# Scores of two of nine steps through the two-bank ring, with one exponential of 1024 columns for two heads

## The chip, the cores and the metric

One core of one Trainium2 chip runs the whole kernel. The metric is device time in microseconds (us) of one execution; the median of three executions stands for the kernel. Engines: PE is TensorE (matmul; PEld its weight loads), DVE is VectorE, ACT is ScalarE, POOL is GpSimd, SP is SyncE, which issues the DMAs.

## What is computed

A transformer block with adaptive layer norm on x of shape (8, 1024, 256), in float32, with 16 heads of 16 channels and windows of 128 keys:

```python
h = layernorm(x) * (1 + ca) + sa
q, k, v = heads(h @ Wq.T + bq), heads(h @ Wk.T + bk), heads(h @ Wv.T + bv)
sc = q @ k.T / 4                               # 1024 x 1024 for each head
# inside each block of 128 keys, and under the causal mask: a softmax of its own
w = exp(sc - max_window(sc)); w = where(causal, w, 0)
w = w / sum_window(w)                          # 0 where the whole window is masked
p = softmax(w, axis=-1)                        # over all 1024 keys, masked ones count as exp(0)
x = x + ga * ((p @ v) @ Wo.T + bo)
h = layernorm(x) * (1 + cb) + sb
y = square(relu(h @ Wfc.T)) @ Wproj.T
x = x + gb * spikes(y) / 5                     # 5 steps of a spiking neuron, as a count of thresholds passed
```

So each score goes through two exponentials, with the window's sum and its inverse between them.

## The kernel before, in words

**Groups, units, steps.** A batch of 1024 tokens has 4 groups of 4 heads (`QH = 4`), 32 groups in all. A group's causal score blocks are cut into `NU = 9` units, each of 512 columns per head (`UNITS`, in transposed form: partitions are the 128 keys of a block, columns are queries). Step n brings the first stage of unit n; n goes to 287 (`NUNIT` = 288), with 14 steps of afterrun. s = n mod 9 is the unit inside the group: s = 0 the first step of a group, s = 8 the last. A batch is 36 steps.

**What runs in step n.** All engines follow the same step number, each with its own instruction stream, tied by semaphores. On TensorE, in this order (`step`, from L879): products of unit n-7 with V (L800, into `pv`); the window sums of unit n-1 (L790, `sum_unit`, which waits until all four first exponentials of step n-1 are done); for unit n-5 the inverse sums spread over the partitions (L829, `one_over_sums`, two calls, each filling one ring slot with two heads of 512 columns); in steps with s = 0 the rest of a mixed unit (`mixed_products`, also L800), ahead of which the first piece goes; then the scores of the four heads, `scores(n, 0..3)` (L775 matmul, L778 adds the causal mask), with other work set between them by tables: `piece` (below), `quantum` (L732, one matmul of the second feed-forward product), `maxima` (L750 and L753, scores in untransposed form of which VectorE takes the window maxima) and `turn_maxima` (L763), which turns the maxima so that SP can put them into the query stack by DMA (they are subtracted inside the score matmul). In step 7 of a group `outputs` (L838) turns the finished outputs.

On ScalarE: the second exponential of unit n-6 (L1046, 128x2048, all four heads), a logarithm and an exponential for the inverse sums (L1052, L1056, in steps divisible by 3), then the first exponentials, one for each head of 512 columns (L1041), with the pieces' evacuations between them. On VectorE: in steps with s = 0 and s = 6 the addition that takes `pv` (L1196), then the two products with the inverse sums, one for each ring slot of two heads (L1180, 128x1024), Newton's step for the inverse (L1184, L1186, steps divisible by 3), and the maxima (L1158), one for each ring slot. POOL splits operands (L1454 to L1458, L1488 to L1494), squares (L1467), counts spikes (L1479, L1481).

**Pieces.** Work of other batches is cut into pieces of one PSUM bank: T1, T2 (transposes before a projection, L664), QK (projections, four matmuls, L688; ScalarE takes them in two copies, L991 and L992), V, BH, BT, AT (turned attention output), O (output projection), F1 (eight matmuls of the first feed-forward product, L720; ScalarE takes it at L1014). The tables FRONT, BACK, NEAR, LATE and FIRST give for each step of a batch a first place (after head 0, or ahead of it where `piece_first`) and a last place (after head 3); QUANTA gives the numbers of quanta after each of the heads.

**PSUM.** There are two ring slots of two banks each (`ring`) and two score banks of one (`score`). Scores, turned maxima and all pieces go through the two score banks in turn: `score_slots` walks the whole order ahead of time and hands each item the bank and the item that held it before; `score_bank` (L644) waits for that item's reader. So head 2 waits for the exponential of head 0 where nothing stands between. The ring is used by the inverse sums (`"r"`, twice a step), the maxima (`"m"`, three a step in s = 1 to 6) and the turned outputs (`"o"`); `RING_NO` numbers them in order, `ring_slot` waits until the item two before was freed by VectorE (`ring_free`). In s = 0 and s = 8 the ring carries nothing but the two of the inverse sums. Semaphores: `st_ready` counts heads whose scores are ready, `e1_done` first exponentials, `ring_ready` filled slots, `ring_free` freed ones.

**SP** issues `load_stacks` for group g (q and k stacks, two DMAs) in step 9(g-1), after all scores of the group that used the same half of the stack.

Steps that the prediction names, with what is placed in them (one batch; the others repeat it every 36 steps):

- s = 8: step 107 F1 after head 0, then 0, 1, 1, 2 quanta after heads 0 to 3; step 116 AT after head 0, AT after head 3, quanta 1, 0, 1, 1; step 125 QK after head 0; step 134 F1 after head 3, quanta 0, 2, 3, 0.
- s = 0: step 108 one quantum after head 3; step 117 AT ahead of head 0, one quantum after head 3; step 126 T2 ahead of head 0 and T2 after head 3; step 135 F1 ahead of head 0 and F1 after head 3.
- at the beginning and the end: step 8 the turned maxima of group 1 between heads 1 and 2; 9, 27, 35, 36 and 269 nothing; 17 and 18 QK; 26 BT; 44 as 116 without quanta; 270 as 126.

## Time and profile before

| | |
|---|---|
| median of three executions | 2356.11 us (2353.27 to 2359.10) |
| the profiled execution | 2358.39 us, its span 2356.6 us |
| TensorE busy | 2206.2 us, 94% of the span |
| VectorE, ScalarE, POOL busy | 74%, 65%, 48% |
| mean granted TensorE clock | 0.99 |
| chain that ended last | PE 77%, DVE 10%, ACT 5%, POOL 4% |

The span runs from the first to the last instruction. A busy TensorE is not TensorE at its peak, since matmuls are pipelined and their ends are modelled. An engine's idle time matters only where the chain that sets the end passes through it; TensorE's waits are therefore what is to be read, and what ended each.

### The profile page before, as it was taken

Reading aid. Unit: us, or ns where it says so; the run is one execution under the profiler, and the core shown is the slowest. Engines: PE = TensorE matmul, PEld = TensorE weight load, DVE = VectorE, ACT = ScalarE, POOL = GpSimd, SP = SyncE. Lnnn points to the kernel's source line nnn. Section 1 sums busy time; section 2 is a strip of 40 time slices with the busy share of each in tenths; the row PEclk is TensorE's granted clock in tenths of the full one; section 3 lists DMA queues with packets and bytes.
Section 4 is the critical chain, followed back from the end, with each engine's and each line's share of the span. In section 5 each row is a group of like instructions: output and inputs, shape, how many; then the busy total and the mean of one; then the engine's idle time right before and its main releaser. Section 6 shows DMA issues by size and latency. Waiting matters only on the chain.

```text
span 2356.6 us, 46649 instructions
## 1 busy us (share of the span) xinstructions
PE 2206.2 (94%) x19164; PEld 1247.1 (53%) x19164; DVE 1753.1 (74%) x2115; ACT 1541.6 (65%) x2157; POOL 1137.6 (48%) x1070
## 2 busy tenths in 40 slices
PE   6889889999999999999998999999999999989988
PEld 4434334455555555455554655545555555545557
DVE  7786887768787676886778777776877767788466
ACT  2477677766667667676777766776666766667741
POOL 3153133545755456644576257653576544443630
PEclk9999999999999999999999999999999999999999
DMA  5233122311122113121133102231022211101000
GB/s 188 62 109 94 48 55 71 94 48 33 54 68 84 52 35 90 41 68 52 35 90 95 47 20 59 66 108 48 8 70 77 84 35 46 39 19 29 6 27 25
DMA packets 114064, 140.20 MB, mean 59 GB/s; under 512 B 8648, under 2 KB 86760, under 8 KB 113856
## 3 DMA queue, kind: packets, MB, share of 16 engines
q1 hardware_dynamic: 113856, 137.23, 20.5%
q8 instruction: 155, 2.54, 0.5%
q14 instruction: 53, 0.43, 0.1%
HBM read 74.26 MB, written 58.74 MB: 56 GB/s over the span
## 4 chain that ended last, share of the span: by engine, by line
PE 77%; DVE 10%; ACT 5%; POOL 4%; issue 2%; DMA 1%; SPq 0%; ACTq 0%; POOLq 0%
PE pv L800 11%; PE ring L750 9%; PE sums L790 9%; PE score L775 9%; PE score L720 9%; PE sums L732 8%; PE score L673 5%; PE score L688 4%; DVE e L1180 4%; PE ring L829 4%; DVE negmax L1158 3%; PE ring L753 2%; PE score L778 2%; PE score L664 2%; ACT e L1041 2%
## 5 line engine op out<-in xcount | busy, mean ns | idle before, releaser
L1041 ACT ACTIVATE e<-score 128x512 f32<-128x512 f32 x1152 | 672.7, 595 | 372.8 <-PE score L778 207.6
L1180 DVE TENSOR_TENSOR e<-ring,e 128x1024 f32<-128x1024 f32 x576 | 681.2, 1224 | 278.1 <-PE ring L829 277.5
L1158 DVE TENSOR_REDUCE negmax<-ring 128x8 f32<-128x1024 f32 x576 | 681.7, 1219 | 150.7 <-PE ring L753 139.4
L1046 ACT ACTIVATE e<-e 128x2048 f32<-128x2048 f32 x288 | 548.6, 1905 | 4.9 <-DVE e L1180 4.9
L775 PE MATMUL score<-q_st,k_st 112*128 112x512 bf16 (+3 forms) x1536 | 459.5, 330 | 57.3 <-ACT e L1041 22.5
L750 PE MATMUL ring<-k_st,q_st 96*128 96x512 bf16 (+3 forms) x1664 | 387.5, 318 | 39.1 <-DVE e L1180 18.1
L1488 POOL TENSOR_SCALAR r_p<-r_b,ab 128x256 bf16<-128x256 f32 x96 | 89.6, 934 | 544.5 <-DVE r_b L1186 544.5
L800 PE MATMUL pv<-e,v 128*17 128x512 f32 (+3 forms) x3072 | 314.4, 497 | 1.3 <-DVE o_t L1196 1.3
L790 PE MATMUL sums<-e,d_ones 128*32 128x256 f32 x4608 | 305.1, 383 | 1.4
L775 PEld LDWEIGHTS score<-q_st,k_st 112*128 112x128 bf16 x1536 | 147.9, 97 | 248.9 <-issue 122.7
L1467 POOL TENSOR_TENSOR gT<-gT 128x512 f32<-128x512 f32 x112 | 117.2, 1051 | 331.5 <-ACT gT L1014 331.5
L732 PE MATMUL sums<-w_proj,gT 128*128 128x256 f32 x896 | 259.3, 394 | 8.1 <-POOL gT L1467 3.7
L720 PE MATMUL score<-hT,w_fc 128*128 128x256 f32 x1024 | 244.2, 383 | 2.7 <-ACT e L1041 1.4
L790 PEld LDWEIGHTS sums<-e,d_ones 128*32 128x32 f32 x4608 | 147.6, 111 | 179.4 <-issue 96.9
L750 PEld LDWEIGHTS ring<-k_st,q_st 96*128 96x128 bf16 x1664 | 150.1, 99 | 147.4 <-DVE negmax L1158 42.4
L753 PE MATMUL ring<-mask_q,id_b 128*128 128x128 bf16 x1024 | 221.5, 221 | 0.0
L720 PEld LDWEIGHTS score<-hT,w_fc 128*128 128x128 f32 x1024 | 189.7, 190 | 33.2 <-ACT e L1041 6.3
L778 PE MATMUL score<-id_b,mask_q 128*128 128x128 bf16 x1024 | 192.3, 220 | 0.0
L732 PEld LDWEIGHTS sums<-w_proj,gT 128*128 128x128 f32 x896 | 148.5, 191 | 38.7 <-DVE r_b L1184 6.6
L1479 POOL TENSOR_SCALAR below<-n 128x512 bf16<-128x512 f32 x104 | 154.9, 1490 | 7.4
L1014 ACT ACTIVATE gT<-score 128x512 f32<-128x512 f32 x112 | 66.9, 597 | 123.4 <-PE score L720 123.4
L753 PEld LDWEIGHTS ring<-mask_q,id_b 128*128 128x128 bf16 x1024 | 100.3, 98 | 53.6 <-issue 3.5
(147 smaller groups left out, 2574.9 us busy)
## 6 DMA issues: line engine op xcount, KB each, us to landing
q_st<-q_parts SPq DMA_DIRECT2D x31, 768.0 KB, 5.9
k_st<-k_parts SPq DMA_DIRECT2D x31, 768.0 KB, 8.6
q_parts<-qk_p SPq DMA_DIRECT2D x30, 384.0 KB, 2.6
k_parts<-qk_p SPq DMA_DIRECT2D x28, 384.0 KB, 2.6
x_in<-in_x SPq DMA_DIRECT2D x8, 1024.0 KB, 5.7
q_parts<-qk_p SPq DMA_DIRECT2D x30, 256.0 KB, 2.9
x_res<-in_x SPq DMA_DIRECT2D x30, 256.0 KB, 4.1
k_parts<-qk_p SPq DMA_DIRECT2D x28, 256.0 KB, 2.9
```

The source lines that it names most:

```text
L720: mm = pe.matmul(ps[:, HALF * i:HALF * i + HALF], w_fc[:, k, P * f:P * f + P], (last_h if r == LB else hT2)[:, k, HALF * c:HALF * c + HALF ...
L732: mm = pe.matmul(sums[:, HALF:HALF + D], gT[:, f, P * i:P * i + P], w_proj[:, f, :], start=(n > NUNIT and f == 0), stop=(f == NF - 1), ski ...
L750: mm = pe.matmul(slot[:, c:stop], q, k_st[0:KROWS, g % 2, hh, c + shift:stop + shift], start=True, stop=not own, skip_group_check=True)
L753: mm = pe.matmul(slot[:, diag:diag + P], id_b[:, :], mask_q[:, :], start=False, stop=True, skip_group_check=True)
L775: mm = pe.matmul(slot[:, c:c + qb - qa], k_st[0:KROWS + MROWS, g % 2, hh, P * j:P * j + P], q_st[0:KROWS + MROWS, g % 2, hh, qa:qb], start ...
L778: mm = pe.matmul(slot[:, c:c + P], mask_q[:, :], id_b[:, :], start=False, stop=True, skip_group_check=True)
L790: mm = pe.matmul(sums[32 * hh:32 * hh + 32, 0:HALF], d_ones[:, 2 * TRI - 1 - row:2 * TRI + 31 - row], e[:, m % ES, hh, HALF * c:HALF * c + ...
L800: mm = pe.matmul(pv[32 * hh:32 * hh + VW, qa - at:qb - at], v1[:, b % 2, j, QH * g + hh, :], e[:, m % ES, hh, c:c + qb - qa], start=start, ...
L1041: act.activation(e[:, n % ES, hh, :], score[SCORE_SLOT["st", n, hh][0]][:, :], ACT.Exp, scale=DK ** -0.5).then_inc(e1_done, 1)
L1046: act.activation(v, v, ACT.Exp).then_inc(e2_done, 1)
L1158: dve.tensor_reduce(negmax[:, hh:hh + heads, at:at + NB // heads], slot[:, :].rearrange("p (h a n) -> p h a n", h=heads, n=P), AX_X, ALU.m ...
L1180: dve.tensor_tensor(v, ring[no % 2][:, :].rearrange("p (i n) -> p i n", i=2), v, ALU.mult).then_inc(ring_free, 1)
```

## The change

A step is *paired* if s is 0 or 8, n < 288, and it has no maxima of its own: 63 steps (all of s = 8, all of s = 0 but n = 0). In these the scores don't go into the score banks but into the ring: heads 0 and 1 into one slot (a bank each), heads 2 and 3 into the next, after the two slots of the inverse sums of the same step. ScalarE takes each slot with one exponential of 1024 columns, which counts 2 on `e1_done`. The next user of such a slot waits on `e1_done` instead of `ring_free` (`RING_ITEM`, `FREE_NO`). `st_ready` no longer counts these steps (`ST_NO`), and `score_slots` has only pieces and turned maxima for them.

The order in a paired step is: first piece, quanta of place 0, heads 0 and 1, turned maxima, quanta of places 1 and 2, heads 2 and 3, last piece, outputs, quanta of place 3. ScalarE follows it: first piece, exponential of heads 0 and 1, turned maxima, exponential of heads 2 and 3, last piece. Places in the tables are now numbered 0 to 3 (after each head); every entry that stood in the last place 1 is now in place 3, so pieces stay in the order they had, and steps that are not paired keep theirs.

```diff
@@ -53,6 +53,8 @@
 PERIOD = NQ * NU
 ES = 7
 LAG_R, LAG_E, LAG_P = 5, 6, 7
+
+PAIRED = (0, 8)
 LAST = NUNIT + 14
 LB = B - 1
 
...
-NEAR = {(39, 0): ("F1", 12), (39, 1): ("F1", 13), (41, 0): ("F1", 14), (41, 1): ("F1", 15)}
+NEAR = {(39, 0): ("F1", 12), (39, 3): ("F1", 13), (41, 0): ("F1", 14), (41, 3): ("F1", 15)}
...
 def placed(n):
 
-    out = [None, None]
+    out = [None] * 4
     b, at = divmod(n, PERIOD)
-    for k in range(2):
+    for k in range(4):
         if b == 0 and (at, k) in FIRST:
...
@@ -216,6 +218,11 @@
     return None
 
 
+def paired(n):
+
+    return n % NU in PAIRED and n < NUNIT and not tiles_of(n)
+
+
 RING_NO = {}
 for _k in range(BEGIN_TILES):
     RING_NO["m", 0, _k] = len(RING_NO)
@@ -225,8 +232,16 @@
             RING_NO["r", _n - LAG_R, _k] = len(RING_NO)
     for _g, _k in tiles_of(_n):
         RING_NO["m", _g, _k] = len(RING_NO)
+    if paired(_n):
+        for _k in range(2):
+            RING_NO["s", _n, _k] = len(RING_NO)
     if turned_out(_n):
         RING_NO["o", turned_out(_n)[0], int(turned_out(_n)[1][0] > 0)] = len(RING_NO)
+
+
+RING_ITEM = list(RING_NO)
+
+FREE_NO = {item: k for k, item in enumerate(item for item in RING_ITEM if item[0] != "s")}
 
 
 def turns(n):
...
     out, held, at = {}, [None, None], 0
     steps = [[*PROLOGUE[:12], ("turn", 0, 0), *PROLOGUE[12:]]]
     for n in range(LAST):
         p = placed(n)
-        st = [("st", n, hh) for hh in range(QH)] if n < NUNIT else [None] * QH
+        st = [("st", n, hh) for hh in range(QH)] if n < NUNIT and not paired(n) else [None] * QH
         turn = ("turn", *turn_of(*turns(n))) if turns(n) else None
+        if paired(n):
+            steps.append([p[0], p[1], turn, p[2], p[3]])
+            continue
         begin = [p[0], st[0]] if piece_first(n) else [st[0], p[0]]
-        steps.append([*begin, st[1], st[2], st[3], p[1], turn] if late_turn(n) else [*begin, st[1], turn, st[2], st[3], p[1]])
+        steps.append([*begin, st[1], p[1], *([] if late_turn(n) else [turn]), st[2], p[2], st[3], p[3], *([turn] if late_turn(n) else [])])
     steps.append(TAIL)
...
@@ -512,6 +534,13 @@
 
             return sum(STEPS if by_vector(k // 4, k % 4) else 2 * STEPS - 1 for k in range(4 * r + c))
 
+        def scores_done(eng, n):
+
+            if paired(n):
+                eng.wait_ge(ring_ready, RING_NO["s", n, 1] + 1)
+            else:
+                eng.wait_ge(st_ready, ST_NO[n] + QH)
+
         block = ctx.enter_context(nc.Block())
 
 
@@ -538,7 +567,7 @@
             def load_stacks(g):
                 b, f0 = g // NQ, QH * DK * (g % NQ)
                 if g >= 2:
-                    sp.wait_ge(st_ready, QH * NU * (g - 1))
+                    scores_done(sp, NU * (g - 1) - 1)
                 for par in range(2):
                     no = QK_NO["QK", b, 4 * (g % NQ // 2) + 2 + par]
...
@@ -654,8 +683,11 @@
 
             def ring_slot(*item):
                 no = RING_NO[item]
-                if no >= 2:
-                    pe.wait_ge(ring_free, no - 1)
+                if no >= 2 and RING_ITEM[no - 2][0] == "s":
+                    _, n, pair = RING_ITEM[no - 2]
+                    pe.wait_ge(e1_done, QH * n + 2 * pair + 2)
+                elif no >= 2:
+                    pe.wait_ge(ring_free, FREE_NO[RING_ITEM[no - 2]] + 1)
                 return ring[no % 2]
 
             def turn(ps, src, n):
...
@@ -769,14 +801,22 @@
                     pe.wait_ge(m_in[hh], 16 * g)
                 elif g == 0 and u in (0, MIXED):
                     pe.wait_ge(first_m_in[int(u == MIXED)][hh], 16)
-                slot = score_bank("st", n, hh)
+                if paired(n):
+                    if hh % 2 == 0:
+                        ring_slot("s", n, hh // 2)
+                    slot = ring[RING_NO["s", n, hh // 2] % 2][:, BANK * (hh % 2):BANK * (hh % 2) + BANK]
+                else:
+                    slot = score_bank("st", n, hh)
                 for (j, qa, qb), c in columns(u):
                     diag = qa == P * j
                     mm = pe.matmul(slot[:, c:c + qb - qa], k_st[0:KROWS + MROWS, g % 2, hh, P * j:P * j + P],
                                    q_st[0:KROWS + MROWS, g % 2, hh, qa:qb], start=True, stop=not diag, skip_group_check=True)
                     if diag:
                         mm = pe.matmul(slot[:, c:c + P], mask_q[:, :], id_b[:, :], start=False, stop=True, skip_group_check=True)
-                mm.then_inc(st_ready, 1)
+                if not paired(n):
+                    mm.then_inc(st_ready, 1)
+                elif hh % 2:
+                    mm.then_inc(ring_ready, 1)
 
             def sum_unit(m):
                 pe.wait_ge(e1_done, QH * (m + 1))
...
@@ -891,20 +931,46 @@
                 if 0 <= n - LAG_R < NUNIT:
                     one_over_sums(n - LAG_R, 0)
                     one_over_sums(n - LAG_R, 1)
-                if piece_first(n) and first:
-                    piece(first)
+                if (piece_first(n) or paired(n)) and p[0]:
+                    piece(p[0])
                 if mixed(n):
                     mixed_products(n - LAG_P)
+                if paired(n):
+                    if p[1]:
+                        piece(p[1])
+                    for item in single[0]:
+                        quantum(n, *item)
+                    scores(n, 0)
+                    scores(n, 1)
+                    if turns(n):
+                        turn_maxima(*turns(n))
+                    for item in single[1]:
+                        quantum(n, *item)
+                    if p[2]:
+                        piece(p[2])
+                    for item in single[2]:
+                        quantum(n, *item)
+                    scores(n, 2)
+                    scores(n, 3)
+                    if p[3]:
+                        piece(p[3])
+                    if turned_out(n):
+                        outputs(*turned_out(n))
+                    for item in single[3]:
+                        quantum(n, *item)
+                    return
                 if -1 in at:
                     maxima(*at[-1])
                 if n < NUNIT:
                     scores(n, 0)
-                if first and not piece_first(n):
-                    piece(first)
+                if p[0] and not piece_first(n):
+                    piece(p[0])
                 for item in single[0]:
                     quantum(n, *item)
...
@@ -1037,11 +1105,21 @@
                     act.wait_ge(pv_done, blocks(n))
                 if hh == 0 and mixed(n):
                     act.wait_ge(mixed_done, (n - LAG_P) // NU + 1)
-                act.wait_ge(st_ready, QH * n + hh + 1)
+                act.wait_ge(st_ready, ST_NO[n] + hh + 1)
                 act.activation(e[:, n % ES, hh, :], score[SCORE_SLOT["st", n, hh][0]][:, :], ACT.Exp, scale=DK ** -0.5).then_inc(e1_done, 1)
 
+            def paired_exp(n, pair):
+                if pair == 0:
+                    act.wait_ge(pv_done, blocks(n))
+                if pair == 0 and mixed(n):
+                    act.wait_ge(mixed_done, (n - LAG_P) // NU + 1)
+                no = RING_NO["s", n, pair]
+                act.wait_ge(ring_ready, no + 1)
+                act.activation(e[:, n % ES, 2 * pair:2 * pair + 2, :], ring[no % 2][:, :].rearrange("p (i n) -> p i n", i=2),
+                               ACT.Exp, scale=DK ** -0.5).then_inc(e1_done, 2)
+
             def second_exp(m):
-                act.wait_ge(ring_free, RING_NO["r", m, 1] + 1)
+                act.wait_ge(ring_free, FREE_NO["r", m, 1] + 1)
                 v = e[:, m % ES, :, :]
                 act.activation(v, v, ACT.Exp).then_inc(e2_done, 1)
...
+                for k in range(2):
+                    if p[k]:
+                        take(p[k])
+                for item in sums_ended(n, 0):
+                    take_sum(*item)
+                paired_exp(n, 0)
+                if turns(n):
+                    take_turned(*turns(n))
+                for item in sums_ended(n, 1):
+                    take_sum(*item)
+                if p[2]:
+                    take(p[2])
+                for item in sums_ended(n, 2):
+                    take_sum(*item)
+                paired_exp(n, 1)
+                if p[3]:
+                    take(p[3])
+                for item in sums_ended(n, 3):
+                    take_sum(*item)
+
+            def by_heads(n, p):
+                if piece_first(n) and p[0]:
+                    take(p[0])
+                if n < NUNIT:
...
```

The rest of the diff renumbers the tables' last place from 1 to 3, puts `FREE_NO` for `RING_NO` wherever `ring_free` is waited for, moves ScalarE's unchanged order into `by_heads`, and lets VectorE look for O pieces in four places.

## Rows read from the trace of the kernel before

**Rows 1.** The page: TensorE's busy time and the exponentials' groups (busy us, mean ns | idle)
```profile
PE 2206.2 (94%) x19164; PEld 1247.1 (53%) x19164; DVE 1753.1 (74%) x2115; ACT 1541.6 (65%) x2157; POOL 1137.6 (48%) x1070
L1041 ACT ACTIVATE e<-score 128x512 f32<-128x512 f32 x1152 | 672.7, 595 | 372.8 <-PE score L778 207.6
L1046 ACT ACTIVATE e<-e 128x2048 f32<-128x2048 f32 x288 | 548.6, 1905 | 4.9 <-DVE e L1180 4.9
```

**Rows 2.** What TensorE waited for: us in total, times, longest us
```profile
PE score L775 <- ACT e L1041: 22.5, 52, 1.4
PE score L775 <- ACT qk_p L992: 18.8, 31, 1.0
PE ring L750 <- DVE e L1180: 18.1, 43, 1.9
PE ring L750 <- DMA k_st<-k_parts: 7.4, 5, 1.9
```

**Rows 3.** Timeline of step 134: start us, us, engine line, [idle before <-releaser]
```profile
1065.88 0.40 PE L829 MATMUL ring<-r_p,sel 32*128 32x256 bf16 x8
1066.31 2.35 DVE L1180 TENSOR_TENSOR e<-ring,e 128x1024 f32<-128x1024 f32 x2 [1.09 <-PE ring L829]
1069.86 1.94 PE L720 MATMUL score<-hT,w_fc 128*128 128x256 f32 x8
```

**Rows 4.** Timeline of step 135
```profile
1073.15 0.40 PE L829 MATMUL ring<-r_p,sel 32*128 32x256 bf16 x8
1075.97 0.39 PE L775 MATMUL score<-q_st,k_st 112*128 112x512 bf16 x1
1078.39 1.99 PE L720 MATMUL score<-hT,w_fc 128*128 128x256 f32 x8 [0.20 <-ACT e L1041]
```

**Rows 5.** Timeline of steps 125 and 126
```profile
999.32 0.40 PE L829 MATMUL ring<-r_p,sel 32*128 32x256 bf16 x8
1003.13 1.80 ACT L1041 ACTIVATE e<-score 128x512 f32<-128x512 f32 x3
1004.99 1.07 PE L790 MATMUL sums<-e,d_ones 128*32 128x256 f32 x16
1005.99 0.40 PE L829 MATMUL ring<-r_p,sel 32*128 32x256 bf16 x8
1009.90 0.66 PE L664 MATMUL score<-id_f,x_in 128*128 128x128 f32 x4
```

**Rows 6.** Timeline of step 116
```profile
929.87 0.40 PE L829 MATMUL ring<-r_p,sel 32*128 32x256 bf16 x8
933.15 0.66 PE L664 MATMUL score<-id_f,tok 128*128 128x128 f32 x4
```

**Rows 7.** Timeline of steps 107 and 108
```profile
862.88 0.70 PE L732 MATMUL sums<-w_proj,gT 128*128 128x256 f32 x2 [0.19 <-POOL gT L1467]
864.93 0.41 PE L829 MATMUL ring<-r_p,sel 32*128 32x256 bf16 x8
868.11 0.70 PE L732 MATMUL sums<-w_proj,gT 128*128 128x256 f32 x2
```

**Rows 8.** Stretches of two steps each (window, us, busy of each engine), and step 8's timeline
```profile
115.51:127.05 11.54, 8.67 (x109) 3.66 (x106) 8.97 (x17) 8.98 (x13) 7.01 (x7) 1.00 0.44 101
248.68:258.58 9.90, 8.37 (x104) 3.51 (x102) 6.16 (x7) 8.16 (x13) 1.07 (x2) 1.00 0.89 238
307.38:317.73 10.35, 8.10 (x102) 3.20 (x98) 8.16 (x15) 8.19 (x13) 6.34 (x6) 1.00 0.62 153
2115.77:2127.01 11.24, 9.45 (x108) 4.00 (x105) 8.16 (x15) 9.54 (x15) 7.15 (x7) 1.00 0.67 149
...
118.72 2.33 DVE L1180 TENSOR_TENSOR e<-ring,e 128x1024 f32<-128x1024 f32 x2
```

**Rows 9.** Two stretches around a fall of the clock (PEclk is the last but two)
```profile
989.60:993.00 3.40, 1.45 (x13) 0.72 (x13) 3.35 (x14) 2.02 (x5) 1.46 (x2) 1.00 0.28 94
993.00:996.40 3.40, 3.40 (x4) 1.38 (x5) 0.79 (x1) 0.58 (x1) 0.00 (x0) 0.50 0.55 180
```

More of the change, by code:

```diff
@@ L263, in piece_first @@
     return mixed(n) or n == max(BEGIN_AT) + 1
+ST_NO = [QH * sum(not paired(k) for k in range(n)) for n in range(NUNIT)]
 def score_slots():
@@ L879, in step @@
             def step(n):
-                first, second = placed(n)
+                p = placed(n)
                 single = quanta(n)
@@ L907, in step @@
                     scores(n, 1)
+                if p[1]:
+                    piece(p[1])
                 if turns(n) and not late_turn(n):
@@ L915, in step @@
                     scores(n, 2)
+                if p[2]:
+                    piece(p[2])
                 if 1 in at:
@@ L923, in step @@
                     maxima(*at[2])
-                if second:
-                    piece(second)
+                if p[3]:
+                    piece(p[3])
                 if 3 in at:
@@ L941, in last_sums @@
                 pe.wait_ge(squared, 16 * LB + 4 * c + 4)
-                pe.wait_ge(ring_free, len(RING_NO) - (1 if c == 0 else 0))
+                pe.wait_ge(ring_free, len(FREE_NO) - (1 if c == 0 else 0))
                 for i in range(2):
@@ L1056, in sum_exp, with in_pairs @@
                 act.activation(r_a[:, :], r_a[:, :], ACT.Exp, scale=-1.0).then_inc(r_exp, 1)
+            def in_pairs(n, p):
+                for k in range(2):
[8 more added lines that the diff above has]
+                    take_sum(*item)
+                if p[2]:
+                    take(p[2])
+                for item in sums_ended(n, 2):
+                    take_sum(*item)
+                paired_exp(n, 1)
+                if p[3]:
+                    take(p[3])
[5 more added lines that the diff above has]
+                if n < NUNIT:
+                    first_exp(n, 0)
+                if p[0] and not piece_first(n):
+                    take(p[0])
+                for item in sums_ended(n, 0):
+                    take_sum(*item)
+                if n < NUNIT:
+                    first_exp(n, 1)
+                if p[1]:
+                    take(p[1])
+                if turns(n) and not late_turn(n):
+                    take_turned(*turns(n))
+                for item in sums_ended(n, 1):
+                    take_sum(*item)
+                if n < NUNIT:
+                    first_exp(n, 2)
+                if p[2]:
+                    take(p[2])
+                for item in sums_ended(n, 2):
+                    take_sum(*item)
+                if n < NUNIT:
+                    first_exp(n, 3)
+                if p[3]:
+                    take(p[3])
+                for item in sums_ended(n, 3):
+                    take_sum(*item)
+                if late_turn(n):
+                    take_turned(*turns(n))
             act.preload_act_table_set("natural_log_exp_and_others")
@@ L1077, in step @@
                 b, s = divmod(n, PERIOD)
-                first, second = placed(n)
+                p = placed(n)
                 t = n // TRI - 1
@@ L1086, in step @@
                     sum_exp(t)
[L1087 to L1112 removed]
+                if paired(n):
+                    in_pairs(n, p)
+                else:
+                    by_heads(n, p)
                 if s == 34 and b + 2 < B:
@@ L1382, in step @@
                     invert(t)
-                first, second = placed(n)
-                if first and first[0] == "O":
-                    take_output(first)
+                p = placed(n)
+                for item in p[:2]:
+                    if item and item[0] == "O":
+                        take_output(item)
                 tiles = tiles_of(n)
@@ L1388, in step @@
                     maxima(g, k)
-                if second and second[0] == "O":
-                    take_output(second)
+                for item in p[2:]:
+                    if item and item[0] == "O":
+                        take_output(item)
                 if turned_out(n):
```

44 lines of the change are left out of this document (9 added, 35 removed).

## The prediction

> **What bounds the kernel now.** I read the page first: TensorE is busy 94% of the span and ScalarE's largest group is the exponential that the change touches [rows 1]. So a change of ScalarE's work counts only where TensorE waits. The waits of TensorE are the second view: it stands idle 22.5 us ahead of score matmuls for an exponential and 18.8 us for the two copies of a QK piece; for VectorE's product in the ring it stands 18.1 us, for the key stack's DMA 7.4 us [rows 2]. Third, the timeline of single steps. Below, t is the start of a step's first L829 matmul (the two fills of the ring with 1/sums); a step lasts from t to the next t. All durations are of the profiled execution (2358.39 us; its span 2356.6), 0.1% above the median 2356.11; the sum is made as a difference and carried to the median.
>
> **What is removed and added.** 63 steps (n mod 9 = 8 or 0, without n = 0) change. Each trades four exponentials of 512 columns (0.595 us) for two of 1024. No row has one; 0.595 and 1.905 us for 2048 columns [rows 1] give 0.85 ns a column, so I estimate 1.03 us, bounded by 0.95 (half of the 2048) and 1.19 (twice 0.595). ScalarE loses 63 x 0.32 = 20 us of work, which by itself buys nothing: it is idle a third of the time. The matmuls stay. What counts is where the scores now wait.
>
> In step 134 VectorE begins its two products 0.43 us after t and needs 2.35 for both [rows 3], so ring slot one is free at t+1.66 and slot two at t+2.78. With 0.06 us from release to matmul (the sums start at 1004.99, the exponentials ended at 1004.93 [rows 5]) heads 0 and 1 can't start before t+1.72, heads 2 and 3 not before t+2.84. Before, head 0 started near t+0.34. A head's issue takes 0.34 us in step 8, 0.29 in step 0. The release time is bounded by 0 and 0.12; in some 41 steps it tells: -2.5 to +2.5 us.
>
> **The price, kind by kind** (each returns once a batch, every 36 steps):
> Step 134 and six like it have no piece or quantum ahead of the scores. TensorE waits from t+0.34 to t+1.72; everything behind, up to the F1 piece (t+3.98 before, [rows 3]), moves by 1.38: loss 7 x 1.38 = 9.7 us.
> Step 135, behind it, has an F1 piece and the mixed products ahead; its scores start at t+2.82, past the release. Four heads end issue at t+3.98, and the second F1 piece, which sat behind two waits on 512-column exponentials until t+5.24 [rows 4], has a score bank of its own free: gain 7 x 1.26 = 8.8.
> Step 125 (QK piece): now the piece goes first, at t+0.33, 0.36 earlier; its copies too. Before, three exponentials followed from 1003.13, t+3.81 [rows 5]; now two long ones from t+3.45 end at t+5.41 (0.1 overlapped), and the sums start at 5.47 instead of 5.67: gain 7 x 0.2 = 1.4. ScalarE is the bound there, so the waits on the QK copies only move behind the scores.
> Step 126 (T2, mixed): scores at t+1.77 and t+2.90, the second T2 at 3.48 where it was 3.91 [rows 5]: gain 6 x 0.43 = 2.6; step 18, QK ahead, 0.4.
> Step 116 (AT, a quantum, AT): TensorE is free at t+1.24, waits to 1.72; heads 2 and 3 issue until 3.59, where the AT piece was at 3.28 [rows 6]: loss 6 x 0.31 = 1.9, and 0.6 in step 44, which has no quanta. Step 117: gain 6 x 0.1 = 0.6.
> Step 107 (F1, quanta): TensorE could be 0.5 us sooner, but its last quantum waits for POOL's square [rows 7], and POOL is in the middle of its spike counts: 0. Step 108 has nothing ahead: its quantum, at t+3.18 [rows 7], goes at 3.42: loss 6 x 0.24 = 1.4.
> Thin steps, without pieces behind the scores: 26 and 27, 35 and 36, 269 and 270, 8 and 9, whose lengths are the stretches of [rows 8]. Here the chain goes on to the sums, which need all four exponentials: heads 2 and 3 end at t+3.69, the last exponential at 4.82, sums at 4.88, and 1.00 more to the next t [rows 5]: 5.88 for step 8, 5.76 for step 0. Losses: 11.64 - 9.90 = 1.7; 11.64 - 10.35 = 1.3; 269 and 270 (two T2 pieces, 5.94), 11.82 - 11.24 = 0.6. In step 8 VectorE is late: its products start at 118.72, t+3.21, and end at t+5.54 [rows 8]; the turn's copy, 1.0 us, stands between the exponentials, so the step takes about 9.3: 15.1 - 11.54 = 3.6. Sum 7.2. Of this 2.2 comes back in steps 10 and 28, where TensorE waits for the key stack's DMA [rows 2], which is issued on SP behind the last head of step 8 or 26 and moves less than TensorE does (it needs no more than that head, and SP has nothing else queued there).
> The long exponential reaches 15 steps (thin and QK), so its bounds give -1.2 to +2.4. In the others the next products cover it. A slot that a pair of scores held is wanted by the next step's 1/sums, over 2 us after its exponential: no cost. Pieces have the score banks to themselves: counted above.
>
> **Sum.** Losses 9.7 + 2.5 + 1.4 + 7.2 = 20.8; gains 8.8 + 1.4 + 2.6 + 0.4 + 0.6 + 2.2 = 16.0. Net 4.8 us slower, 2363.2 for the profiled execution, 2360.9 against the median: 0.2%. A measurement of this kernel can tell about 0.3% (7 us) from no change, so the likeliest verdict is no difference.
>
> **Two rules of the Trainium skill.** The rows say that ScalarE, at 65%, is not saturated, and that its exponentials do make TensorE wait [rows 1, 2]. The Trainium skill (Perfetto Trace Analysis, Optimizing Scalar/DVE Operations) says that grouping helps a saturated engine, and that breaking up instructions helps where an unsaturated one causes bubbles; by it this change is the wrong way round, as the thin steps above have it (the second rival). The Trainium skill (ScalarE: Activation LUTs, Rules for kernel authors) budgets about 0.3 us an ACTIVATE and 0.83 ns an element; the rows give 0.16 fixed (0.595 less 512 x 0.85 ns), so the trace disagrees. By its figures the two long exponentials behind the QK copies cost 0.11 us more than three short ones, not 0.27, and the sum would be 1.1 us less.
>
> **Rivals.** (a) Faster, chance 0.13: TensorE's 18.1 us of waits on VectorE's products in other steps [rows 2], and those on its reductions, absorb what is lost, because TensorE comes later to a slot that is free at a fixed time. If two thirds of the 20.8 go, 6.9 - 16.0 = -9: 2347. It decides only if VectorE is behind; but in step 134 VectorE starts 0.1 us after its matmul, having idled 1.09 [rows 3], and such waits are chains that begin at TensorE.
> (b) Slower, 0.22: step 135 gives nothing back. Its gain rests on the second F1 going at once and nothing being late next. If ScalarE (its 2048-column exponential, then the F1 copy) or POOL's squares hold the next steps' products or quanta by 1.26 us, the 8.8 is gone: 2369.7. It decides if the sums of step 136 or a quantum waits. Against: the four exponentials end near t+5.6, the products are reached at t+5.9.
> (c) Slower still, 0.08: TensorE's clock. A stretch of 3.4 us with 1.45 busy was followed by one granted 0.50, that is 1.2 GHz of 2.4 [rows 9]. Step 134 would have 1.38 us idle in a row, the thin steps more. If each of seven such waits brings one, at 1.7 us: +11.9, 2373. Against: 1.38 idle leaves about 2.0 of 3.4 busy.
> The forecast has 0.57.
>
> **Numbers.** From the forecast's bounds (-2.5 to +2.5, -1.2 to +2.4, the kinds' own error of some 3): 2355 to 2368 in its own right. The whole range, 2349 to 2371, takes in most of (a)'s near side and (b). Faster by over 0.3%: (a), 0.12. Slower by over 0.3%, above 2363.2: (b), (c) and 0.1 of the forecast, 0.40. Within: 0.48.
>
> **What would show it.** Exponentials of 1024 columns, 126, of 1.03 us; TensorE's waits on L1041 down by some 17 us, those on the QK copies before L775 down by 7, and new ones of L775 on VectorE's L1180, 1.4 us long in steps like 134, 0.5 in 116 and 108; the second F1 of step 135 at t+4.0; step 126 at 5.9, step 35 at 5.9 instead of 4.3. I am wrong if L775 hardly waits on L1180, if steps 1 to 7 shorten, if step 135 stays at 9.0, or if the clock's mean falls.

## The result, and the profile after

| | before | changed |
|---|---|---|
| median | 2357.45 us (4 runs) | 2377.20 us (2374.69 to 2378.75, 4 runs) |
| ratio, 95% interval | | 1.0082 (1.0069 to 1.0095) |
| the profiled execution, its span | 2358.39, 2356.6 us | 2376.11, 2374.3 us |
| mean granted TensorE clock | 0.990 | 0.986 |

The changed kernel is 0.8% slower, 20 us where 4.8 were forecast; the span of the profiled execution grew by 17.7. The rest, 2 us, is scatter between executions; what follows reads the 17.7.

The page after. Code has moved: the first exponentials are now L1109 (by heads) and L1118 (1024 columns); the second one is L1124, before L1046.

```profile
PE 2200.6 (93%) x19164; PEld 1250.8 (53%) x19164; DVE 1759.5 (74%) x2115; ACT 1528.4 (64%) x2031; POOL 1137.6 (48%) x1070
...
L1109 ACT ACTIVATE e<-score 128x512 f32<-128x512 f32 x900 | 531.0, 595 | 315.9 <-PE score L815 160.4
...
L1118 ACT ACTIVATE e<-ring 128x1024 f32<-128x1024 f32 x126 | 127.3, 1024 | 81.2 <-PE ring L815 78.4
```

The exponential of 1024 columns takes 1.024 us, and 126 of them replace 252. ScalarE has 13 us less to do, TensorE is busy for 6 us less, and the span is longer: TensorE waits more. What TensorE waited for (us in total, times, longest), to be set against [rows 2]; L812 are the scores (before L775), L1289 VectorE's product (L1180), L782 the maxima, L696 the transposes (L664):

```profile
PE ring L812 <- DVE e L1289: 42.2, 66, 4.1
PE ring L782 <- DVE e L1289: 18.8, 45, 1.9
...
PE sums L830 <- ACT e L1118: 11.9, 17, 1.2
PE score L812 <- ACT qk_p L1060: 11.1, 23, 0.6
...
PE score L812 <- ACT e L1109: 5.6, 15, 0.7
PE score L696 <- DVE x_in L1389: 4.8, 6, 0.8
```

The waits of the scores on ScalarE went, from 22.5 to 5.6 us and, behind the QK copies, from 18.8 to 11.1. In their place stand 42.2 us on VectorE's product, 11.9 us of the window sums (L830) on the long exponential (8.7 of it in the seven steps 125 and like, behind the QK copies), and 4.8 us of T2 pieces on a normalisation (`x_in`), where it was 0.6 us before. The length of each step (t to t), after less before, says where that counts. It repeats from batch to batch to within 0.05 us where the clock does not fall, but for one step: 117 itself is 0.49 longer and the five like it 0.21, since its second long exponential starts 0.28 us later than in them, and no row says why.

| steps | forecast each | measured each | forecast, all | measured, all |
|---|---|---|---|---|
| 134 and like (7) | +1.38 | +1.32 | +9.7 | +9.2 |
| 135 and like (7) | -1.26 | -1.36 | -8.8 | -9.5 |
| 125 and like (7) | -0.20 | -0.16 | -1.4 | -1.1 |
| 126 and like (6), 18 | -0.43, -0.4 | +0.65, -0.55 | -3.0 | +3.8 |
| 107 and like (6) | 0 | 0 | 0 | 0 |
| 108 (6) | +0.24 | +0.54 | +1.4 | +3.2 |
| 116 (6), 44 | +0.31, +0.6 | +0.24, +0.58 | +2.5 | +2.0 |
| 117 and like (6), 45 | -0.1, 0 | +0.21, 0 | -0.6 | +1.5 |
| 26 and 27 | +1.7 | +1.80 | +1.7 | +1.8 |
| 35 and 36 | +1.3 | +2.36 | +1.3 | +2.4 |
| 269 and 270 | +0.6 | +0.50 | +0.6 | +0.5 |
| 8 and 9 | +3.6 | +5.23 | +3.6 | +5.2 |
| 10 and 28 (DMA) | | -1.1, -0.8 | -2.2 | -1.9 |
| all others | 0 | | 0 | +0.6 |

Steps 134 and 135, timeline of the changed kernel, against [rows 3] and [rows 4]:

```profile
1077.26 0.40 PE L869 MATMUL ring<-r_p,sel 32*128 32x256 bf16 x8
1077.69 2.36 DVE L1289 TENSOR_TENSOR e<-ring,e 128x1024 f32<-128x1024 f32 x2 [1.09 <-PE ring L869]
1078.97 0.34 PE L812 MATMUL ring<-q_st,k_st 112*128 112x384 bf16 x1 [1.31 <-DVE e L1289]
...
1082.55 1.94 PE L752 MATMUL score<-hT,w_fc 128*128 128x256 f32 x8
```

```profile
1085.85 0.41 PE L869 MATMUL ring<-r_p,sel 32*128 32x256 bf16 x8
1088.66 0.39 PE L812 MATMUL ring<-q_st,k_st 112*128 112x512 bf16 x1
1089.78 1.94 PE L752 MATMUL score<-hT,w_fc 128*128 128x256 f32 x8
1093.51 0.40 PE L869 MATMUL ring<-r_p,sel 32*128 32x256 bf16 x8
```

Step 134: the scores start 1.71 us after t, having waited 1.31, 0.06 after the first product; the F1 piece comes at t+5.29 where it was at 3.98. Step 135: scores at t+2.81, the second F1 at 3.93 where it was at 5.24, the step 7.66 long. These two meet the forecast to 0.1 us.

Step 126 does not. Steps 125 and 126, against [rows 5]; L1060 is the second QK copy (before L992), L1389 VectorE's normalisations (L1280), L1565 the first part of POOL's split (L1454). Two lines of before, in which step 125 began at 999.32, and then the changed kernel:

```profile
1002.83 3.15 DVE L1280 TENSOR_SCALAR x_in<-x_res,mv,rstd 128x256 f32<-128x256 f32 x4
1003.32 1.26 POOL L1454 TENSOR_TENSOR qk_p<-qk_f,qk_p 128x512 bf16<-128x512 f32 x1 [1.63 <-ACT qk_p L992]
```

```profile
1010.21 0.40 PE L869 MATMUL ring<-r_p,sel 32*128 32x256 bf16 x8
1013.16 0.68 ACT L1060 ACTIVATE qk_p<-score,b_qk 128x512 bf16<-128x512 f32 x1
1013.72 4.05 DVE L1389 TENSOR_SCALAR x_in<-x_res,mv,rstd 128x256 f32<-128x256 f32 x4
1013.91 1.24 POOL L1565 TENSOR_TENSOR qk_p<-qk_f,qk_p 128x512 bf16<-128x512 f32 x1 [1.33 <-ACT qk_p L1060]
1016.72 0.40 PE L869 MATMUL ring<-r_p,sel 32*128 32x256 bf16 x8
1017.92 0.63 PE L696 MATMUL score<-id_f,x_in 128*128 128x128 f32 x4 [0.80 <-DVE x_in L1389]
1018.30 2.34 DVE L1289 TENSOR_TENSOR e<-ring,e 128x1024 f32<-128x1024 f32 x2
1019.65 0.38 PE L812 MATMUL ring<-q_st,k_st 112*128 112x512 bf16 x1 [0.55 <-DVE e L1289]
1020.78 0.38 PE L812 MATMUL ring<-q_st,k_st 112*128 112x512 bf16 x1 [0.42 <-DVE e L1289]
1021.33 0.60 PE L696 MATMUL score<-id_f,x_in 128*128 128x128 f32 x4
```

The scores of step 126 go at t+2.93 and t+4.06 where 1.77 and 2.90 were forecast, and the second T2 at t+4.61 instead of 3.48. Ahead of them the first T2 waited 0.80 us for VectorE's normalisations, which took 4.05 us for four, and VectorE's products themselves start only 1.58 us after t. The order of events in step 125: the second QK copy ends 3.63 us after t (0.3 us earlier than before), so POOL starts at 3.70; before, it started at 4.00. VectorE's four normalisations start at 3.51 in both kernels. One by one they take 0.42, 0.41, 1.25 and 1.33 us in the trace of before, and 0.41, 1.25, 1.32 and 1.31 in that of the changed kernel. The second starts 3.84 us after t, which is before POOL's start in the one and behind it in the other. Each that starts once POOL is at work takes three times as long.

### The profile page after: what moved, and what is told of

Read it like the earlier page. It is cut to its first block, busy times and chain, and to the rows that moved or that the text cites. A ratio compares the mean times of both kernels' runs of the same rounds, so it can differ in the third digit from the quotient of the medians.

```text
span 2374.3 us, 46555 instructions
## 1 busy us (share of the span) xinstructions
PE 2200.6 (93%) x19164; PEld 1250.8 (53%) x19164; DVE 1759.5 (74%) x2115; ACT 1528.4 (64%) x2031; POOL 1137.6 (48%) x1070
## 4 chain that ended last, share of the span: by engine, by line
PE 76%; DVE 13%; POOL 4%; ACT 3%; issue 2%; DMA 1%; SPq 0%; ACTq 0%; POOLq 0%
PE pv L840 10%; PE sums L830 9%; PE ring L782 9%; PE score L752 8%; PE sums L764 8%; PE score L812 7%; DVE e L1289 7%; PE score L705 5%; PE score L720 4%; PE ring L869 4%; DVE negmax L1267 3%; PE ring L785 2%; PE ring L812 2%; PE score L815 1%; POOL below L1590 1%
## 5 line engine op out<-in xcount | busy, mean ns | idle before, releaser
L1289 DVE TENSOR_TENSOR e<-ring,e 128x1024 f32<-128x1024 f32 x576 | 681.1, 1224 | 275.3 <-PE ring L869 274.9
L1109 ACT ACTIVATE e<-score 128x512 f32<-128x512 f32 x900 | 531.0, 595 | 315.9 <-PE score L815 160.4
L1124 ACT ACTIVATE e<-e 128x2048 f32<-128x2048 f32 x288 | 549.1, 1907 | 2.8 <-DVE e L1289 2.8
L782 PE MATMUL ring<-k_st,q_st 96*128 96x512 bf16 (+3 forms) x1664 | 387.0, 317 | 38.2 <-DVE e L1289 18.8
L812 PE MATMUL score<-q_st,k_st 112*128 112x512 bf16 (+3 forms) x1156 | 358.6, 337 | 27.2 <-ACT qk_p L1060 11.1
L830 PE MATMUL sums<-e,d_ones 128*32 128x256 f32 x4608 | 306.7, 384 | 13.0 <-ACT e L1118 11.9
L830 PEld LDWEIGHTS sums<-e,d_ones 128*32 128x32 f32 x4608 | 146.1, 111 | 197.4 <-issue 89.7
L782 PEld LDWEIGHTS ring<-k_st,q_st 96*128 96x128 bf16 x1664 | 149.8, 98 | 146.3 <-DVE negmax L1267 41.1
L812 PEld LDWEIGHTS score<-q_st,k_st 112*128 112x128 bf16 x1156 | 111.1, 97 | 153.7 <-issue 58.0
L1118 ACT ACTIVATE e<-ring 128x1024 f32<-128x1024 f32 x126 | 127.3, 1024 | 81.2 <-PE ring L815 78.4
L812 PE MATMUL ring<-q_st,k_st 112*128 112x384 bf16 x380 | 91.6, 314 | 42.2 <-DVE e L1289 42.2
```

The source lines that it names most:

```text
L782: mm = pe.matmul(slot[:, c:stop], q, k_st[0:KROWS, g % 2, hh, c + shift:stop + shift], start=True, stop=not own, skip_group_check=True)
L812: mm = pe.matmul(slot[:, c:c + qb - qa], k_st[0:KROWS + MROWS, g % 2, hh, P * j:P * j + P], q_st[0:KROWS + MROWS, g % 2, hh, qa:qb], start ...
L830: mm = pe.matmul(sums[32 * hh:32 * hh + 32, 0:HALF], d_ones[:, 2 * TRI - 1 - row:2 * TRI + 31 - row], e[:, m % ES, hh, HALF * c:HALF * c + ...
L1109: act.activation(e[:, n % ES, hh, :], score[SCORE_SLOT["st", n, hh][0]][:, :], ACT.Exp, scale=DK ** -0.5).then_inc(e1_done, 1)
L1124: act.activation(v, v, ACT.Exp).then_inc(e2_done, 1)
L1289: dve.tensor_tensor(v, ring[no % 2][:, :].rearrange("p (i n) -> p i n", i=2), v, ALU.mult).then_inc(ring_free, 1)
```

## Experiments

Theory A, after this reading: 126's loss is VectorE's normalisations slowed by POOL's split, which starts earlier because the QK piece goes ahead of the scores; the rest is waiting for VectorE's release. Theory B: the ring or the long exponential is itself too slow in step 126. Theory C: the long exponential is the main cost. The times are medians, set against the kernel before; that stood at 2357.6 to 2358.2 beside them.

**Only the steps s = 0 paired.** `PAIRED = (0,)`.

> Only the steps with s = 0 are paired. Theory A (step 126 got 0.65 us longer, not 0.43 shorter, because the QK copies of step 125 came 0.3 us earlier, so POOL's split ran into one more of VectorE's four normalisations, and the T2 piece and both ring slots of step 126 came late): with step 125 as before, step 126 and its five like get 0.43 us shorter than before; 135 stays 1.36 shorter, 108 is 0.5 and 117 0.2 longer. Sum about -9 us against the kernel before, 2348. Theory B (the ring or the long exponential is itself too slow in step 126): it stays 0.65 longer, the sum is about -2, 2355.

Measured: 2352.26, ratio 0.9978 (0.9969 to 0.9988). Step 126 and like are 0.42 us shorter than before, 135 is 1.36 shorter, 108 0.54 and 117 0.21 longer, as theory A has it. The time is 4 us above the forecast. Step 36 is 1.47 longer: VectorE's products start late there, at t+1.34 as before the change, when 35 isn't delayed (which the expectation left out), and a fall of the clock stands in that step too. Some unpaired steps move with the clock.

**Only the steps s = 8 paired.** `PAIRED = (8,)`.

> Only the steps with s = 8 are paired. All of their loss stays (134 +1.32, 116 +0.24, 8 +5.3, 35 +2.6). Theory A: step 126, though not paired, is longer by some 0.8 us, its T2 waits for VectorE's normalisation. Sum +23 us, 2380. Theory B: step 126 is as before, sum +17, 2375. In both step 135 is as before, so the gain there needs no pairing in 134.

Measured: 2381.73, ratio 1.0097 (1.0081 to 1.0113). Step 126, not paired and with 512-column exponentials, is 0.84 longer, and its T2 waits as long as in the changed kernel:

```profile
1019.81 0.63 PE L696 MATMUL score<-id_f,x_in 128*128 128x128 f32 x4 [0.80 <-DVE x_in L1389]
```

So neither the ring nor the long exponential of step 126 is needed for its loss; theory B falls. Step 135 is as before: its gain is its own, and 134's loss buys nothing for it. Step 117 and like, not paired here either, are 0.45 longer behind the paired 116, which the expectation did not have.

**The kernel before, with the QK piece ahead of head 0, and nothing else.**

```diff
-    return mixed(n) or n == max(BEGIN_AT) + 1
+    return mixed(n) or n == max(BEGIN_AT) + 1 or n % PERIOD == 17
```

> The kernel before, with nothing paired; only the QK piece of steps 17, 53, 89, ... 233 goes ahead of head 0 instead of behind it. Theory A: POOL's split starts about 0.3 us earlier, a further normalisation of VectorE in step 125 takes 1.25 us instead of 0.41, T2 of step 126 waits about 0.8: step 126 and its five like 0.8 to 1.0 longer, 125 within 0.1; about +5 us, 2362. Theory B: step 126 is unchanged, the time within 1 us of before.

Measured: 2364.77, ratio 1.0031 (1.0020 to 1.0041), 7 us slower. By the steps 4.5 us of it are the order of one piece in seven steps; steps 88 and 232 are 1.7 longer each by falls of the clock. Timeline of its steps 125 and 126 (lines as before the change):

```profile
1001.39 0.40 PE L829 MATMUL ring<-r_p,sel 32*128 32x256 bf16 x8
1004.90 4.06 DVE L1280 TENSOR_SCALAR x_in<-x_res,mv,rstd 128x256 f32<-128x256 f32 x4
1005.09 1.24 POOL L1454 TENSOR_TENSOR qk_p<-qk_f,qk_p 128x512 bf16<-128x512 f32 x1 [1.63 <-ACT qk_p L992]
...
1009.11 0.63 PE L664 MATMUL score<-id_f,x_in 128*128 128x128 f32 x4 [0.24 <-DVE x_in L1280]
```

POOL starts at t+3.70, the four normalisations take 4.06 us: the same as in the changed kernel, without any pairing. Of the loss 0.41 falls in step 125 (four short exponentials behind the copies) and 0.27 in 126, where the expectation had 0.1 and 0.8 to 1.0; T2's own wait is 0.24 and not 0.8, since 125 ends later. So the run shows the slower normalisations, and not the size of the loss in 126.

**The changed kernel without the QK steps paired.** `and n % PERIOD != 17` in `paired`.

> The changed kernel, but steps 17, 53, ... 233 (QK) are not paired. Theory A: step 125 +0.16 against the changed kernel, step 126 goes from +0.65 to -0.43 against before (1.08 less): 5.5 us less than the changed kernel, 2371.5, give or take 2 for falls of the clock. Theory B: no change in step 126, 2378.

Measured: 2368.02, ratio 1.0043 (1.0030 to 1.0056), 9 us less than the changed kernel; step 126 is at -0.41 against before, as theory A has it. More than forecast: the condition also frees step 269 (1.6 less, of which 270 gives 0.9 back), and some falls of the clock went.

**The changed kernel with POOL waiting for VectorE** in the QK steps, so that only the overlap is taken away:

```diff
                     piece_done(pool, *item)
+                    if at is not None and 2 <= at // PERIOD < B and at % PERIOD == 17 or at == PERIOD + 17:
+                        pool.wait_ge(xn2[0], 4 * (at // PERIOD))
```

> The changed kernel; in steps 53, 89, ... 233 POOL's split of the QK piece waits until VectorE's four normalisations are done, so that the two never run at once. Theory A: all four take 0.41 us (done at t+5.1 instead of t+7.6), the T2 of step 126 waits for nothing, its ring slots are free at t+1.7 and 2.8, step 126 goes from +0.65 to about -0.4 against before; POOL is some 1.5 us late and nobody waits for it. 6.5 us less than the changed kernel, 2370 to 2372. Theory B: step 126 keeps +0.65.

Measured: 2370.07, ratio 1.0052 (1.0039 to 1.0065). Timeline of steps 125 and 126:

```profile
1011.45 1.38 DVE L1389 TENSOR_SCALAR x_in<-x_res,mv,rstd 128x256 f32<-128x256 f32 x4
1012.97 1.16 POOL L1567 TENSOR_TENSOR qk_p<-qk_f,qk_p 128x512 bf16<-128x512 f32 x1 [2.67 <-DVE x_in L1389]
...
1014.78 0.66 PE L696 MATMUL score<-id_f,x_in 128*128 128x128 f32 x4
```

All four normalisations take 1.38 us together, POOL starts at t+5.03 instead of 3.70, T2 goes without a wait, and step 126 is 0.47 us shorter than before: a swing of 1.12 us for 1.3 us of delay on POOL. Theory A is shown from both sides: the order of the piece alone slows the normalisations, and taking away the overlap alone gives the time back.

**Short exponentials out of the ring.** Each head's matmul signals, and two exponentials of 512 columns take a slot (a semaphore for the even heads, `ACT.Exp` on `ring[no % 2][:, BANK * i:BANK * i + BANK]`).

> As the changed kernel, but each ring slot is taken with two exponentials of 512 columns, each released by its own head. Theory A (waiting for VectorE's release is the loss, the long exponential a small part): step 134 stays 1.3 longer, 126 stays 0.65 longer; thin steps (26, 27, 35, 269) lose 0.4 each of their loss, 108 and 117 0.1 to 0.3, 125 gets 0.1 longer. 5 us less than the changed kernel, 2372. Theory C (the long exponential is what costs): 12 us less or more, 2365 and below, with step 126 back.

Measured: 2376.57, ratio 1.0082 (1.0069 to 1.0095), no less than the changed kernel. By steps it did what theory A has: 134 stays at +1.32, 108 goes to +0.26, 117 to -0.06, 26 from +0.88 to +0.54; step 126 changed little, +0.54. Its step 108 (L1092 is the copy of the sum, L833 the window sums):

```profile
872.21 0.40 PE L872 MATMUL ring<-r_p,sel 32*128 32x256 bf16 x8
876.59 0.39 ACT L1092 ACTIVATE n<-sums 128x256 f32<-128x256 f32 x1
877.14 1.05 PE L833 MATMUL sums<-e,d_ones 128*32 128x256 f32 x16
```

Over the steps in which neither kernel has a fall, this is 5 us less than the changed kernel. The time shows none of it: the record of the granted clock has 74.8 us at the half clock, against 69.0 in the changed kernel and 51.5 before, and that nothing would be left I did not foresee. Theory C, 12 us and step 126 back, falls; the length of the exponential is the smaller part.

**Quanta of place 1 ahead of heads 0 and 1.**

```diff
-                    for item in single[0]:
+                    for item in single[0] + single[1]:
```

> The changed kernel, but in paired steps the quanta of place 1 go ahead of heads 0 and 1. If step 134's loss is the idle time up to the release of the first ring slot, two quanta (0.92 us) fill it and its +1.32 falls to +0.4; 107 and 116 stay. 6.4 us less than the changed kernel, 2371. If the loss is the pairing of the heads or what comes behind it, step 134 keeps its +1.3.

Measured: 2374.26, ratio 1.0069 (1.0056 to 1.0081). Its step 134:

```profile
1077.02 0.40 PE L869 MATMUL ring<-r_p,sel 32*128 32x256 bf16 x8
1077.35 1.13 PE L764 MATMUL sums<-w_proj,gT 128*128 128x256 f32 x4
1078.73 0.34 PE L812 MATMUL ring<-q_st,k_st 112*128 112x384 bf16 x1 [0.25 <-DVE e L1287]
```

Two quanta fill the gap, the wait shrinks from 1.31 to 0.25, the step goes from +1.32 to +0.46: the loss was the idle time up to the release. Yet the kernel gained 3 us instead of 6.4: the record shows 89.8 us at the half clock, with falls in steps 26, 90, 162, 198, 234, 269 and 282 that the changed kernel doesn't have.

**No thin steps paired.** `n not in (8, 9, 26, 27, 35, 36, 269, 270)`.

> The changed kernel, but steps 8, 9, 26, 27, 35, 36, 269 and 270 are not paired. By the trace of the changed kernel these give back 9.9 us and take away 1.9 that the DMA waits of steps 10 and 28 had absorbed: 8 us less, 2369. The falls of TensorE's clock in step 8 and step 35 (matmuls of 0.50 us instead of 0.34) should go too; the ones in steps 124, 160, 196, 232 come at a fixed distance and may stay or go, 1.2 to 1.7 us each.

Measured: 2372.78, ratio 1.0062 (1.0050 to 1.0075). The eight steps are as before to 0.01 us and their two falls of the clock are gone, but 69.0 us at the half clock remain, in other places. 4 us gained of 8.

**The sum's last quantum and its copy ahead of the scores**, in paired steps s = 0 (`single[0] + single[3]`, and `sums_ended(n, 3)` before the first exponential).

> The changed kernel; in paired steps with s = 0 the quantum of place 3, which ends a sum, and ScalarE's copy of it go ahead of the scores. If steps 108 and 117 lose because the copy stands behind the second long exponential and the window sums wait for it, the window sums then wait for the exponential alone: 108 from +0.54 to +0.15, 117 from +0.21 to -0.1, 4 us less in all. If they lose by the ring alone, 108 stays at about +0.5.

Measured: 2399.68, ratio 1.0180 (1.0166 to 1.0194), a miss: 108 is 1.88 longer than before, 117 1.56. Its step 108:

```profile
879.01 0.40 PE L869 MATMUL ring<-r_p,sel 32*128 32x256 bf16 x8
882.18 0.70 PE L764 MATMUL sums<-w_proj,gT 128*128 128x256 f32 x2 [2.21 <-DVE r_b L1293]
...
882.92 0.38 ACT L1089 ACTIVATE n<-sums 128x256 f32<-128x256 f32 x1 [2.94 <-PE sums L764]
```

In steps divisible by 3 a quantum waits for VectorE's Newton step (`r_newton`), which comes behind both products, at t+3.1. I had read the order of the code and not this wait. The whole queue of TensorE, the scores too, stood behind it. So the run does not test what it was made for.

**What gained, alone.** `return n % PERIOD in (18, 27) and 54 <= n < NUNIT`.

> Paired only where a piece and the mixed products stand ahead of the scores: steps 126 and 135 of each batch (n mod 36 = 18 or 27, from n = 54 on), 14 steps. Theory A: 135 and like -1.36, 126 and like -0.43, 270 -1.1, the rest as before: -13 us, 2344. Theory B: 126 +0.65, -5 us, 2352.

Measured: 2349.24, ratio 0.9963 (0.9950 to 0.9975). By the steps 135 and like (-9.5) and 126 and like (-2.7) are as theory A has it. That is 12.2, of which the medians show 8.9; 58.9 us at the half clock stand against 51.5 before.

**The same with 17 (from 53 on) and 9, POOL's wait, and the quantum ahead.**

> A version out of what gained: paired are 17, 18, 27 and 9 (mod 36, from n = 53 on, without 269), with POOL's wait and the quantum ahead. 135 -1.36, 126 -0.4, 125 -0.16, 117 -0.1: 15 us less than before by the steps, of which the clock's falls may take 2 to 4: 2345.

Measured: 2354.41, ratio 0.9983 (0.9974 to 0.9991), where 2345 was forecast: steps 117 and like lost 1.56 each by the wait shown above; without the quantum ahead they lose 0.21, as in the run with s = 0 alone.

**17, 18 and 27, with POOL's wait.** `return n % PERIOD in (17, 18, 27) and 53 <= n < NUNIT and n != 269`; the line that puts a quantum ahead stayed in, but steps 126, 135 and like have no quantum.

> As the version with 126 and 135 paired (2349.2), and with step 125 paired too, POOL waiting there: 125 -0.16 and 126 another -0.05, six times each, 1.3 us less: 2348. The steps 117, which the last version lengthened by 1.56 each since a quantum ahead of the scores waits for VectorE's Newton step, are as before: 7 to 9 us less than that version. Falls of the clock may move it by 3 either way.

Measured: 2344.37, ratio 0.9949 (0.9936 to 0.9962). The best of these kernels: 0.5% faster than before, 1.4% faster than the changed one. Step 135 -1.36, 126 -0.47, 125 -0.16.

## Why the prediction was wrong

The sign of its net and most of its terms held; the measured time lies 6 us above its range. In the profiled executions 17.7 us stand against 4.8, and the 13 missed come from three steps of the working (6.8, 3.9 and some 3 us; the other terms came out 1 us better than forecast).

**The gain in 126, 6.8 us of the 13 missed** (0.5 of it a fall of the clock in step 54). The prediction had -0.43 for each; it measured +0.65. It took from step 125 that "its copies too" come 0.36 us earlier and booked it as a gain. It followed the copies' reader on TensorE, not the one on POOL, and it took VectorE's start in step 126 from the trace of before as fixed. POOL's split comes 0.3 us sooner, makes one more of VectorE's normalisations three times as long, and 0.9 us of delay is handed on to T2, to the addition that takes `pv`, and to both ring slots. The trace of before has the 1.25 us beside the 0.41: it was there to read. The Trainium skill (SBUF — State Buffer, Who interferes with whom) says that VectorE's two-port operations and GpSimd share a pair of ports, as an exclusive lock for a whole instruction. This case's runs agree (0.41 us alone, 1.25 to 1.33 beside POOL); that the normalisation is such an operation no run here shows.

**The cover at 108 and 117, 3.9 us.** "In the others the next products cover" the long exponential: true of the exponential alone, but behind it on ScalarE's queue stands the copy of the sum's last quantum (L1089), and the window sums wait for that as well. Step 108 of the changed kernel, against [rows 7]:

```profile
875.03 0.40 PE L869 MATMUL ring<-r_p,sel 32*128 32x256 bf16 x8
876.83 0.38 PE L812 MATMUL ring<-q_st,k_st 112*128 112x512 bf16 x1 [0.84 <-DVE e L1289]
...
878.51 0.65 PE L764 MATMUL sums<-w_proj,gT 128*128 128x256 f32 x2
879.69 0.38 ACT L1089 ACTIVATE n<-sums 128x256 f32<-128x256 f32 x1
880.21 1.07 PE L830 MATMUL sums<-e,d_ones 128*32 128x256 f32 x16
881.21 0.40 PE L869 MATMUL ring<-r_p,sel 32*128 32x256 bf16 x8
```

The scores go at t+1.80 and 2.93 (0.08 later than I had it), the quantum at 3.48 instead of 3.42. By an estimate from step 108 of before (products to sums, 0.87 us) the sums could start near t+4.95, but the copy ends at 5.04 and they start at 5.18. With short exponentials out of the same ring the copy ends at 4.77 and the sums start at 4.93, and the steps 108 and 117 get 0.27 or 0.28 shorter each: that shows the length of the exponential as the cause of 3.3 us of the 3.9. That the copy is what hands it on is read from the rows, since the run that moved the copy failed.

**The clock, some 3 us,** which the prediction had as a rival at 8%, priced for the seven waits like step 134's; of the thin steps it said only that they have more idle time. Step 8 and stretches around it:

```profile
120.20 0.50 PE L812 MATMUL ring<-q_st,k_st 112*128 112x384 bf16 x1 [4.05 <-DVE e L1289]
...
115.74:119.20 3.46, 0.40 (x12) 0.12 (x8) 3.27 (x11) 0.00 (x0) 1.72 (x2) 1.00 0.00 0
119.20:126.69 7.49, 6.31 (x50) 3.30 (x50) 2.76 (x3) 4.54 (x4) 3.30 (x3) 0.54 0.05 15
```

After 3.5 us with 0.40 busy, the matmuls of the scores take 0.50 us instead of 0.34; TensorE was at 1.2 of its 2.4 GHz. The step took 10.95 us, 5.34 longer, where 3.7 was forecast; in the run with POOL's wait it has half as long a fall (3.4 us for 6.8) and takes 10.34. Step 35, with a fall too, took 6.88 us where 5.88 was forecast; in the run with POOL's wait it has no fall and takes 5.96, and 26 and 269, like it and without one, were met to 0.02. The falls also come in steps that the change leaves alone. Step 160 (s = 7), before and after, and two stretches of it in the changed kernel:

```profile
1270.43:1279.93 9.50, 7.14 (x72) 3.56 (x69) 6.63 (x17) 5.99 (x11) 4.06 (x5) 1.00 0.30 99
1282.78:1293.52 10.74, 8.42 (x73) 4.09 (x70) 6.63 (x17) 5.99 (x11) 4.06 (x5) 0.84 0.27 88
1283.30:1286.70 3.40, 1.53 (x14) 0.75 (x12) 3.32 (x14) 1.70 (x3) 2.42 (x2) 1.00 0.00 0
1286.70:1290.10 3.40, 2.95 (x5) 1.31 (x6) 1.75 (x2) 1.48 (x3) 0.00 (x0) 0.51 0.80 262
```

The same work takes 10.74 us where it took 9.50. Its instructions and waits are those of before, the wait for the turned maxima among them; only their place in time moved, and here a fall follows. Why it falls in one and not in the other no run here settles. Steps 124, 160, 196 and 232 all have one in the changed kernel, 124 and 196 before. In the row "all others" of the table steps 16, 33 and 43 are 4.6 us shorter without the falls that they had, and 24, 52, 88, 160 and 232 are 7.3 us longer with new ones. The prediction looked for the clock in the places where the edit puts idle time; each kernel here has its falls in other steps, and the experiments' times lie 3 us and up to 6 from the sums of their steps. None of the seven steps like 134, where rival (c) looked for them, has one in the changed kernel.

**Right:** the release of the ring slots as the new bound and its price in 134 and 116, the gain in 135 (rival (b) did not come, and neither did (a): the maxima wait 18.8 us for VectorE's products where it was 18.1), the thin steps without a fall, the part that the DMA waits absorb, the duration of the exponential (1.024 for 1.03). ScalarE's saved time bought nothing by itself. The Trainium skill (Perfetto Trace Analysis, Optimizing Scalar/DVE Operations) says that breaking up instructions may help where an unsaturated engine causes bubbles. It points the right way, by the smaller part: of the 11.9 us of new waits for the long exponential 8.7 stand in the QK steps, which got shorter all the same, and the short exponentials gave back 5 us by the steps. The larger part is the slot, not the size of the instruction.

**One reading to set right.** The prediction says that the trace disagrees with the 0.3 us an ACTIVATE of the Trainium skill (ScalarE: Activation LUTs, Rules for kernel authors). That figure is given there for a bias that is read as an operand, which these exponentials don't have; the QK copy, which has one (`b_qk`), takes 0.68 us for 512 columns, and the exponential 0.595. By the two figures as the prediction uses them the difference is an estimate of 0.12 us, not 0.11. Back to back, two long exponentials took 1.94 us in step 125, and three short ones 1.80 before.

## What to carry to other kernels

Moving work to another buffer changes whom it waits for: look up the time at which that buffer is free in each step and compare it with the time at which the work was ready; where something else stands ahead (135, 126) the move is free and removes a wait, where nothing does (134, 8, 35) it costs the whole difference, which other work set ahead can fill (134, from 1.32 to 0.46). So make such a change per step and keep those that gain: two kinds of steps gave 0.4%, three 0.5%, all of them lost 0.8%. An event that comes earlier is not a gain by itself: ask on every engine what it now overlaps with, VectorE and GpSimd above all.

## What the runs showed of the hardware

- A VectorE normalisation of 128x256 in float32 takes 0.41 us alone, 1.25 to 1.33 while GpSimd runs its split; 0.3 us of earlier start on GpSimd cost 0.9 us on VectorE, and 1.3 us of delay on GpSimd cost TensorE nothing.
- Two kernels, or two batches of one, with the same instructions in a step differ by 1.2 us in it when the granted clock falls there. The sum over a run was 51.5 us at the half clock before and 47 to 90 in the kernels here, without a TensorE instruction added or taken away.
- ScalarE's exponential of 1024 columns out of two banks takes 1.024 us, and two in a row 1.94: the second starts 0.91 us after the first.
